# Tokens of the first tiles read from the second norm's buffers, a second set of buffers for gathered rows, and a last pair of batches joined and stored one by one

## What is computed

```python
x = x + jnp.tanh(g_xattn[0]) * _L0_xattn_ref(_layernorm(x, axis=-1), ctx_512, ctx_512)
x = x + jnp.tanh(g_ffn[0]) * _L0_ffn_ref(_layernorm(x, axis=-1), ...)

def _moe_forward(x, ...):          # N = 4096 tokens, H = I = 512, 7 routed experts, the best 2 of each token
    gate = (xt @ Wr + br) / TEMP
    _, ids = jax.lax.top_k(gate + gate_bias, TOPK)
    probs = softmax over the two chosen
    u = jnp.einsum('nh,ehi->eni', xt, Wup) + bup[:, None, :]
    g = jax.nn.silu(jnp.einsum('eni,eij->enj', u, Wgate) + bgate[:, None, :]) * u
    eo = jnp.einsum('enj,ejh->enh', g, Wdown) + bdown[:, None, :]
    out = jnp.einsum('ne,enh->nh', probs, eo)
    su = xt @ Wsu + bsu ; sg = silu(su @ Wsg + bsg) * su ; so = sg @ Wsd + bsd      # the shared expert
    return out + so
```

## Time and profile before

| | us |
|---|---|
| median of 3 runs | 1282.55 (1279.67 to 1288.29) |
| the profiled execution | 1292.41 |
| its span, first to last instruction | 1290.7 |
| outside its span | 1.7 |
| PE busy | 1208.5 (94%) |
| DVE busy | 850.5 (66%) |
| ACT busy | 585.4 (45%) |
| POOL busy | 377.2 (29%) |
| HBM read and written over the span | 308 GB/s |

### The profile page before, as it was taken

One profiled execution on the slowest core, in us unless ns is written; L12 is line 12 of the kernel. 1 busy time (PEld: TensorE's weight loads), 2 busy tenths in 40 slices (PEclk: granted clock), 3 DMA queues, 4 the chain that ended last, 5 costly groups with the idle time before them and its releaser, 6 DMA issues.

```text
span 1290.7 us, 40530 instructions
## 1 busy us (share of the span) xinstructions
PE 1208.5 (94%) x15170; PEld 891.8 (69%) x15170; DVE 850.5 (66%) x1470; ACT 585.4 (45%) x1131; POOL 377.2 (29%) x454
## 2 busy tenths in 40 slices
PE   3878889999879999999999999999999999998998
PEld 2444445555357777778888888888888888876675
DVE  5879889999777799444555454444444444447887
ACT  3768778989787322233333333333333333322221
POOL 4557756666720000211110111111111101015652
PEclk9979889999989999999999999999999999999999
DMA  5665456555665131744221553116411142267674
GB/s 188 217 227 173 174 173 201 200 200 201 240 229 170 66 131 66 256 147 163 99 72 66 165 184 122 65 65 220 138 65 57 57 151 77 79 193 237 222 227 135
DMA packets 91601, 197.36 MB, mean 153 GB/s; under 512 B 12176, under 2 KB 12688, under 8 KB 91536
## 3 DMA queue, kind: packets, MB, share of 16 engines
q1 hardware_dynamic: 80816, 161.34, 36.3%
q0 software_dynamic: 10720, 35.14, 9.1%
HBM read 332.72 MB, written 64.49 MB: 308 GB/s over the span
## 4 chain that ended last, share of the span: by engine, by line
PE 75%; DVE 11%; issue 5%; DMA 3%; POOL 2%; ACT 1%; DVEq 1%; SPq 0%; ACTq 0%; POOLq 0%
PE PS L1649 42%; PE PS L1687 20%; DVE negm L999 5%; PE PS L1634 3%; PE PS L1469 3%; PE PS L1503 2%; DMA qB<-negT 2%; PE PS L1489 1%; DVE xn L985 1%; DVE wst L1028 1%; DVE rec L1012 1%; ACT x2n L870 1%; POOL whl L687 1%; PE PS L1511 1%; PE PS L1517 1%
## 5 line engine op out<-in xcount | busy, mean ns | idle before, releaser
L1649 PE MATMUL PS<-xT,wb 128*128 128x128 f16 (+1 forms) x4128 | 282.7, 230 | 8.2 <-issue 6.4
L1649 PE MATMUL PS<-uhl,wb 128*128 128x128 f16 (+1 forms) x4128 | 283.6, 229 | 1.2 <-DVE uhl L1253 1.2
L1649 PEld LDWEIGHTS PS<-xT,wb 128*128 128x128 f16 x4128 | 265.0, 98 | 19.4 <-issue 9.7
L1649 PEld LDWEIGHTS PS<-uhl,wb 128*128 128x128 f16 x4128 | 264.1, 98 | 13.2 <-DVE uhl L1253 1.4
L1687 PE MATMUL PS<-wb,ghl 128*128 128x512 f16 x1200 | 267.2, 379 | 0.0
L1687 PEld LDWEIGHTS PS<-wb,ghl 128*128 128x128 f16 x1200 | 116.0, 98 | 130.1
L914 ACT ACTIVATE sl<-PS,bb 128x128 f32<-128x128 f32 (+1 forms) x344 | 106.6, 387 | 193.6 <-PE PS L1649 184.3
L904 ACT ACTIVATE u<-PS,bb 128x128 f32<-128x128 f32 (+1 forms) x344 | 106.7, 387 | 176.0 <-PE PS L1649 170.1
L1260 DVE TENSOR_TENSOR g<-sl,u 128x512 f32<-128x512 f32 x102 | 70.3, 689 | 174.1 <-ACT sl L914 173.4
L738 POOL COPY ixr<-idx 128x2 int32 (+1 forms) x35 | 6.4, 183 | 599.2 <-PE PS L1634 599.2
L999 DVE TENSOR_REDUCE negm<-PS 128x8 f16<-128x1024 f32 x128 | 155.2, 1213 | 26.5 <-PE PS L1469 25.8
(11 more groups left out here) (156 smaller groups left out, 1436.3 us busy)
## 6 DMA issues: line engine op xcount, KB each, us to landing
wb<-wsc SPq DMA_DIRECT2D x219, 1024.0 KB
wst<-in_wall SPq DMA_DIRECT2D x32, 768.0 KB, 5.9
wsc<-whl SPq DMA_DIRECT2D x32, 768.0 KB, 4.3
ysl<-yb SPq DMA_DIRECT2D x43, 512.0 KB
bd<-in_bdown SPq DMA_DIRECT2D x74, 256.0 KB
X<-in_x SPq DMA_DIRECT2D x8, 1024.0 KB, 6.7
qB<-qT SPq DMA_DIRECT2D x32, 256.0 KB, 2.9
xnd<-xhl SPq DMA_DIRECT2D x32, 256.0 KB, 2.0
```

Of the source, the lines that this page charges most:

```text
L1649: ins = pe.matmul(bank_of(bank, t, m, kind), wb[:, j, l, k, w, m * P:(m + 1) * P], rhs(x, k)[:, ts], start=(n == 0), stop=(n == len(TERMS) ...
```

## The change

It has four parts, three of them at the two ends of the tiles.

1. **First tiles.** The groups of the second norm are taken in the order 1, 2, ..., 7, 0 (`group_of`), so that the batches 0 to 3 are the last in the four buffers `xhl`. `tr_x` of tiles 0 and 1 transposes straight from these buffers; their loads from `xnd` are gone, and SP's queue has the eight groups' stores with only the weight store among them. The loads of tiles 2 and 3 come behind all stores. `tr_x(0)` stands ahead of the gate logits of the last batch, the last two rounds have no `warm`, and DVE's `evac_x(0, 0)` stands ahead of `logits`.
2. **Gathered rows.** A second tensor `yh` of the size of `yg` (in memory that the routed tiles' first weight buffer has left free), so that there are buffers for four pieces. Gathers of piece m wait for piece m - 4.
3. **Pieces.** They are done later, by a table (`PIECES`), and the DVE's late tiles are written out instead of looped.
4. **The end.** In the last tile, each batch's `down_out` is followed at once by its `shared_last`, and each batch is stored by itself (256 KB).

```diff
+        with ExitStack() as behind:
+            yh = sb("yh", [P, 4, 2, HID], F32, behind)
+        YG = [yg, yh]
...
+        def group_of(i):
+            return (i + 1) % (NB // 4) if isinstance(i, int) else i + 1
...
             store_w(NB // 2 - 1, 1, True)
-            sp.wait_ge(S["x1_ready"], NB)
-            for i in range(2):
-                for r in range(4):
-                    sp.wait_ge(x2_out[r], 16)
-                load_x(i, i, 2 * i)
-                store_x2(3 + i)
-            with sp.Fori(5, NB // 4) as i:
+            with sp.Fori(3, NB // 4 - 1) as i:
                 store_x2(i)
+            store_x2(NB // 4 - 1)
             for par in range(2):
                 load_bias(E_R, par, 0, always)
+            sp.wait_ge(S["x1_ready"], NB)
+            for i in range(2, 4):
+                load_x(i, i % 2, 2 * i)
...
-            put(NB // 4 - 1, 1)
+            for t in range(2):
+                sp.wait_ge(added[1], 2 * (NB // 4) - 1 + t)
+                sp.dma_start(out[NB - 2 + t], ob[:, 2 + t, :]).then_inc(o_out[1], 16)
...
-            def fetch(n):
+            def fetch(n, s, first):
                 for par in range(2):
-                    if not isinstance(n, int):
-                        g.wait_ge(added[par], 2 * n)
+                    if not first:
+                        g.wait_ge(added[par], 2 * n - 2)
                         g.nop(nofuse=True)
...
+            for s in range(2):
+                fetch(s, s, True)
+            with g.Fori(1, NB // 8) as m:
+                for s in range(2):
+                    fetch(2 * m + s, s, False)
...
+            PIECES = [[[], [], [0]], [[1], [], [2]], [[3], [], [4]], [[5], [], [6]], [[7], [], [8]],
+                      [[9], [10], [11]], [[12], [13], [14]]]
...
+            evac_x(0, 0)
             logits()
-            evac_x(0, 0)
...
-                down_out(i, par, kind, half)
                 if following is None:
-                    shared_last(late, i, par)
+                    for t in range(2):
+                        down_out_one(i, par, kind, half, t)
+                        shared_last(late, i, par, t)
...
+                    if last and k == 3:
+                        pe.wait_ge(S["exp_done"], UNITS * NB)
+                        pe.wait_ge(S["att_ready"], 2 * NB)
+                        tr_x(0, 0, "early", 0)
                     gates(i, k)
-                    warm()
+                    if not last or k < 2:
+                        warm()
```

More of the change, by code:

```diff
@@ L209, in program @@
         scat = [sem(f"scat{j}") for j in range(2)]
-        yg_in = [sem(f"yg_in{j}") for j in range(2)]
+        yg_in = [[sem(f"yg_in{s}{j}") for j in range(2)] for s in range(2)]
         ys_in = [sem(f"ys_in{j}") for j in range(2)]
@@ L437, in load_x @@
             def load_x(i, par, b):
-                need(sp, S["xt_done"], 2 * i - 2)
+                if not (isinstance(i, int) and i < 4):
+                    need(sp, S["xt_done"], 2 * i - 2)
                 for t in range(2):
@@ L764, in fetch @@
                         for t in range(2):
[L765 to L770, removed]
+                            g.indirect_dma_start(out=YG[s][:, 2 * par + t, k, :], out_offset=None, in_=ysl,
+                                                 in_offset=bass.IndirectOffsetOnAxis(ap=ixf[:, at + t, k:k + 1], axis=0)).then_inc(yg_in[s][par], 16)
+            for s in range(2):
[3 more added lines that the diff above has]
+                    fetch(2 * m + s, s, False)
         @block.scalar
@@ L882, in _ @@
             act.wait_ge(S["ln2_ready"], 3)
-            for k in range(4):
-                norm2(NB // 4 - 1, k, False)
+            for i in range(NB // 4 - 2, NB // 4):
+                for k in range(4):
+                    norm2(i, k, False)
             def evac_x(i, par):
@@ L1386, in tile @@
                     add_shared(early, ys[:, par, :])
-                if isinstance(late, int) and late == 1:
-                    add_routed(1, 0)
-                elif isinstance(late, int) and late == 2:
-                    add_routed(2, 1)
-                down_out(i, par, kind, half)
-                if following is None:
-                    shared_last(late, i, par)
+                if late is not None and following is not None:
+                    add_pieces(PIECES[late][1])
+                if following is None:
+                    for t in range(2):
+                        down_out_one(i, par, kind, half, t)
+                        shared_last(late, i, par, t)
+                else:
+                    down_out(i, par, kind, half)
                 if late is not None and following is not None:
@@ L1397, in tile @@
                         add_shared(EARLY + 2 * late + t, yb[:, par, t, :])
[L1398 to L1401 removed]
+                    add_pieces(PIECES[late][2])
             for par in range(2):
@@ L1422, in _ @@
                 tile(SH_B0 // 2 + 1, par, "late", "late", late=1 + par)
-            with v.Fori(SH_B0 // 2 + 2, N_TILES // 2) as h:
+            for h in range(SH_B0 // 2 + 2, N_TILES // 2):
                 for par in range(2):
@@ L1601, in _, with tr_x @@
             tr_x2(0, 0)
+            def tr_x(i, par, kind, half):
+                own = isinstance(i, int) and i < 2
+                if not own:
+                    come, count = tokens(kind, half, par)
+                    pe.wait_ge(come[par], count)
+                for t in range(2):
+                    if own:
+                        pe.wait_ge(S["x2l_ready"], NB - 3 + 2 * i + t)
+                    need(pe, S["xTv_ready"] if t else S["xTa_ready"], i)
+                    if t == 1 and isinstance(i, int) and i == 3:
+                        pe.wait_ge(S["rnk_read"], 1)
+                    src = PS[3][:, t, :].bitcast(F16).rearrange("p (n c) -> p n c", c=P)
+                    for n in range(2 * KT):
+                        rows = xhl[:, 2 * i + t, n // KT, (n % KT) * P:(n % KT + 1) * P] if own else xs[:, par, t, n * P:(n + 1) * P]
+                        ins = pe.transpose(src[:, n, :], rows, id16[:, :])
+                    ins.then_inc(S["xt_done"], 1)
             def four(i, last):
@@ L1623, in ranks @@
                 pe.matmul(CNT.rearrange("p b e -> p (b e)"), one16[:, :], mv, start=True, stop=True).then_inc(S["rt_cnt"], 1)
-            def tr_x(i, par, kind, half):
-                come, count = tokens(kind, half, par)
-                pe.wait_ge(come[par], count)
-                for t in range(2):
-                    need(pe, S["xTv_ready"] if t else S["xTa_ready"], i)
-                    if t == 1 and isinstance(i, int) and i == 3:
-                        pe.wait_ge(S["rnk_read"], 1)
-                    src = PS[3][:, t, :].bitcast(F16).rearrange("p (n c) -> p n c", c=P)
-                    for n in range(2 * KT):
-                        ins = pe.transpose(src[:, n, :], xs[:, par, t, n * P:(n + 1) * P], id16[:, :])
-                    ins.then_inc(S["xt_done"], 1)
             TERMS = [(w, x, k) for w, x in ((0, 0), (0, 1), (1, 0)) for k in range(KT)]
```

82 lines of the change are left out of this document (38 added, 44 removed).

## The result

The changed kernel takes 1275.09 us (median of 14 runs), the kernel before 1283.11 beside it (14 runs): a ratio of 0.9936, interval 0.9920 to 0.9953, so 6.0 to 10.3 us less, 8.0 by the medians. The forecast was 10.7 less. The profiled execution came to 1273.47 us, 19 us less than the one before.

A forecast was written before the change was run, and what follows sets the result against it. The kernel was taken as matmul bound (PE busy 94%), gaining only at PE's holes; - 7.3 - 1.15 - 0.25 - 2.0 - 0 = - 10.7 us takes the median from 1282.55 to 1271.9 us, range 1264 to 1281.

The forecast's parts named there:

- the likeliest case: Whole kernel: the forecast itself, 10.7 us less, median 1271.9 us, own range 1268.5 to 1275; chance 0.45.
- rival (a): Tile 45: unprofiled, the pause is only 2.7 us and the clock stays up; 6.1 us less, 1276.5 us; chance 0.22.
- The pause of tile 45, 7.3 us: Tile 45: PE's 4.85 us wait for gathered rows and 2.43 us of slower matmuls both go; bounds 2.7 and 7.3.
- of tile 46, 1.15: Tile 46: half of a 2.28 us loss, put down to DMA traffic piled up behind tile 45's pause, goes.
- rival (d): Stretch 1155 to 1225: back-to-back gathers crowd the DMA engines and starve PE; 4.1 us slower, 1286.7 us; chance 0.07.
- Rival (b): Tile 46: its loss belongs to the return of PE's loop and stays; 9.55 us less, 1273.0 us; chance 0.10.
- The end, - 0.25: Last tile: joins save 0.6 us, the shorter store 0.95, and the later last gating costs 1.3.
- The last gating: Last tile: DVE's three-piece tiles make its gating 1.3 us late, PE's 0.3 us stop included; bounds 0.7 and 2.7.
- two waits of 1.90: Tiles 48 and 49: DVE's idle 1.90 us before the second `down_out` hides part of a 2.65 us piece.
- The second norm, - 2.0: Second norm: of ACT's 2.37 us wait for a store to `xnd`, 2.0 us go; bounds 0.5 and 2.4.
- The turn to tile 0: Start of tile 0: earlier transposes are offset by logits and memsets behind the copy; 0 us, bounds - 0.8 and + 0.4.
- my 0.95 from 262 GB/s: Last store: 256 KB instead of 512 at the profile's 262 GB/s saves 0.95 us; bounds 0.4 and 1.3.

The follow-up runs named there:

- e1_first: Only part 1 (first tiles) added to the kernel before: 1284.31 us, ratio 1.0001 (0.9980 to 1.0023).
- e4_last: Only part 4 (the end) added to the kernel before: 1283.21 us, ratio 1.0000 (0.9979 to 1.0022).
- e2_buffers: Only part 2 (buffers for four pieces, old places, DVE's late tiles written out) added to the kernel before: 1282.33 us, ratio 0.9991.
- e10_places: The whole change with the three-piece tiles at 46 and 48 instead of 48 and 49: 1274.98 us, ratio 0.9936 to the kernel before.
- e7_all_again: The whole change measured once more against the kernel before: 1276.33 us, ratio 0.9937 (0.9913 to 0.9961).
- e6_no_first: The whole change without part 1, against the kernel before: 1276.24 us, ratio 0.9945 (0.9923 to 0.9968).
- e11_places_no_first: The whole change without part 1, three-piece tiles at 46 and 48: 1275.48 us, ratio 0.9933 to the kernel before.
- e9_memsets: The whole change with the logits' two memsets ahead of the copy of tile 0's tokens: 1273.19 us, ratio 0.9922 to the kernel before.
- e3_later: Only part 3 (later places, buffers for two pieces only) added to the kernel before: 1284.76 us, ratio 1.0011.

## Why the prediction was right, and where it was not

**The direction, the place and the range held.** 1275.09 lies in 1264 to 1281 and just beyond the likeliest case's own 1268.5 to 1275; a change of less than one per cent was the likeliest class. The size is three quarters of the forecast. The measured 1275.09 lies nearer to rival (a)'s 1276.5 than to my 1271.9.

**The 19 us of the two profiles.** By the table, 1.8 us of them lie ahead of the norm and 3.65 in tiles 0 to 42, where the matmuls are the same. The kernel before stands alone there with 734.84; the other six profiles without part 1 have 731.1 to 731.8. So its execution was an unlucky one, and perhaps in 2 us of its late tiles too (143.60 against 141.89 for e1_first, which has the same late code). This is some 5 us of the 9.9 between its time and the median, on which rival (a) rested; where the rest lies is not shown. That the pauses come only with a profile is unlikely: the profiled executions of e1_first and e4_last, 1283.9 and 1280.99 us, lie at and under their kernels' medians, 1284.31 and 1283.21, and have them.

**The pause of tile 45, 7.3 us, and of tile 46, 1.15.** Their sum is right, in part by luck. With the pieces at their old places and two buffers, three profiles lose 9.6 us (before), 8.1 (e1_first) and 5.5 (e4_last) in these two tiles, 7.7 on the mean; I had 8.45, worked out from the one that lost most. How it is divided was wrong. In tile 45 PE stood 4.85 us in the profile before and only 1.77 and 2.14 us in the other two, with 5.41 us for the 48 matmuls behind: this is the mild pause with the clock up of rival (a).

The step that failed is the reading of tile 46. I put its 2.28 us down to crowded DMA engines, and counted half. The profiles of e1_first and e4_last, with the same code there, show in tile 46 a pause of 4.58 and of 3.01 us in front of the up layer, with DVE waiting for gathered rows. The chain of e1_first, and its POOL and DVE:

```profile
1179.15 1.77 issue
1180.92 5.41 PE PS L1661 x48
...
1197.65 4.58 issue
1202.23 6.79 PE PS L1661 x48
```

```profile
1187.85 0.18 POOL L764 COPY ixf<-pos 128x4 int32 x1 [0.74 <-DVE ob L1304]
...
1192.70 1.02 POOL L770 DMA_INDIRECT yg<-ysl,ixf  x1 [0.30 <-issue]
...
1198.69 1.42 DVE L1304 SCALAR_TENSOR_TENSOR X<-yg,prb,X 128x512 f32<-128x512 f32 x2 [3.27 <-DMA yg<-ysl,ixf]
```

It is piece 6. Its gathers start 0.74 us late for want of a buffer, those of pieces 4 and 5 started without such a wait, and those of piece 2 had waited 2.73 us; so the two buffers and POOL's rate both have a share. e2_buffers, where POOL never waits for a buffer, still pauses 3.70 us for this piece, so the rate alone is enough. In the profile before, the long pause of tile 45 gave POOL 7 us more, and this wait did not show. So tile 45's pause and tile 46's are one loss, and when the first is mild the second is long, which rival (a) left out. I had POOL's rate, and followed it only through the new order; through the old one, with four buffers, it would have said that part 2 alone cannot win.

What made the gaps inside the run of matmuls of tile 46 in the profile before stays open. They stand in no other of the fourteen profiles. The changed kernel ran the stretch 1198 to 1207 at a DMA share of 0.88 (the last column but one) with PE busy throughout, which speaks against rival (d):

```profile
1198.00:1207.00 9.00, 9.00 (x69) 5.88 (x67) 6.81 (x12) 1.86 (x3) 6.93 (x7) 1.00 0.88 301
```

Rival (b), the loop's return, falls: PE's loop is the same in all kernels, and tile 46 is clean in all ten profiles with part 3.

**The end, - 0.25.** Better by half a microsecond. The joins and the shorter store gave 1.3 us, where I had 1.55: from the second `down_out` to the end of the span it is 5.3 us in each of the five profiles without part 4 and 4.0 in each of the nine with it. The last gating came 0.5 us late, not 1.3: from tile 48's transposes to it 37.99 us before (1239.60 to 1277.59), 38.5 now (1221.43 to 1259.93). PE did not pause in tile 49, where I had 0.3. DVE's backlog takes back idle time that I had left out. The stretches from tile 48's transposes to this gating, before and now (DVE's busy time is the third):

```profile
1239.60:1277.59 37.99, 37.99 (x319) 29.63 (x317) 33.19 (x54) 9.59 (x20) 18.05 (x21) 1.00 0.59 183
```

```profile
1221.43:1259.93 38.50, 38.50 (x326) 30.11 (x324) 37.96 (x62) 9.72 (x21) 19.32 (x21) 1.00 0.65 208
```

DVE stood idle 4.80 us there before and stands idle 0.54 now, so 4.26 us of the added work are hidden; I had counted two waits of 1.90. e10_places fits: 0.5 us of the backlog was to be had, and 0.6 came.

**The second norm, - 2.0.** In the profiles it is there: 57.5 us on the mean of seven without part 1, 55.2 on the mean of the four with part 1 and the old memsets, 2.3 less, about the size of the wait. (I had written that one wait in the norm is long. There are two; the earlier one, 2.40 us in the profile before, is 1.3 to 2.8 us in the seven profiles with part 1, which does not touch it.) In time it is not there. Three pairs differ by part 1 alone: e1_first and before (+ 0.01%), e7_all_again and e6_no_first (- 0.08%), e10_places and e11_places_no_first (+ 0.03%). Their mean is zero, with some 0.15%, 1.9 us, to either side, so that 2.3 us are just excluded and 1 us is not. This term, at 2.0 us, is the largest miss of the sum: without it the forecast is 8.7 us, beside the 8.0 measured. The other two nearly cancel, some 0.7 us too much for the pauses by the mean of three profiles, and 0.5 too little for the end. Where the 2.3 us go is open. The start of the norm moves by 7.7 us from one profile to another (349.3 to 357.0) and is 1.2 us later on the mean with part 1, which fourteen executions do not tell from chance; so it may be that the attention's end gives back what the norm wins, and no run separates the two. The turn to tile 0, counted at 0 by its two opposed steps, was 0 to 0.2 us, released by L1152 as forecast, and e9_memsets turned the step against it into 0.7.

For the shorter store the prediction named the page "DMA: Bandwidth & Descriptors" of the Trainium skill, section "Anatomy of one DMA — SWDGE (gpsimd) path": by its 436 GB/s the half would be worth 0.6 us, an estimate. The joins take 0.54 us of the 1.3 (from the second `down_out` to the last join's end 2.02 us before, 1285.40 to 1287.42, and 1.48 now, 1267.74 to 1269.22), so some 0.75 are left for the store: between that estimate and my 0.95 from 262 GB/s. A fixed cost of the second DMA did not show in the total.

## What to carry to other kernels

When a buffer wait goes, work out the producer's rate next: a gather queue of 6.4 us a piece cannot keep up with three pieces in each tile of 16.55 us however many buffers there are, unless it has run ahead, as it has when the three-piece tiles come last. And a later place in the consumer's order is worth nothing without the buffers that let the producer run ahead. Two parts that show nothing alone can give all together, so test them in pairs. And take the sum of a change from stages of several profiles: one pair of them showed 19 us here where the timed runs showed 8.

## What was not expected of the hardware

- The same code for tiles 0 to 42 took 734.84 us in one profile and 731.0 to 732.4 in thirteen: 192 matmuls of a routed tile took 10.84 us there and 10.72 elsewhere, at a granted clock of 1.00 from 600 to 760 us in both. The cause is open.
- The attention ahead of the norm, the same code in all, spread over 7.7 us.
- A piece, four gathers of 256 KB and the copy of their row numbers, takes POOL 5.7 to 6.9 us (e2_buffers); the rows land 3.6 to 5.75 us behind the end of the last issue (pieces 2 and 3 of the profile before), 4.6 in e2_buffers (1191.51 to 1196.15).
- Behind PE's pauses of 1.77 us (e1_first), 2.14 and 3.01 (e4_last) and 2.36 (e3_later) the 48 matmuls took 5.41 us each time, at a granted clock of 1.00. Behind 3.70 (e2_buffers), 4.58 (e1_first) and 4.85 (before) they took 6.97, 6.79 and 7.67, at a mean clock of 0.77, 0.79 and 0.69, and behind 3.41 (e3_later) the last 24 took 8.23 instead of some 5.5, at 0.65.
